# Between gated attention and first experts: the steps of four engines put in a new order, chunk by chunk

## The reference, cut to what matters

```python
x = x + layernorm(L1_attn(layernorm(x)))   # gated attention: sigmoid(s - mu) * exp(s), normalised
x = x + layernorm(L1_ffn(layernorm(x)))    # gated unit: (silu(x @ Wg) * (x @ Wu)) @ Wd, 384 hidden
x = x + layernorm(L2_attn(layernorm(x)))   # linear attention with elu + 1 features, proj, then
                                           # its own LayerNorm, fc1 (512), exact gelu, fc2, residual
x = x + layernorm(L2_ffn(layernorm(x)))    # 16 experts, 4 of them per token, and a shared one
```

## Time and profile before

| | us |
|---|---|
| median of 3 runs (1506.9 to 1511.1) | 1508.39 |
| the profiled execution | 1511.61 |
| its span in the profile | 1509.7 |
| PE busy in the span | 1274.5 (84%) |
| DVE busy | 1133.8 (75%) |
| ACT busy | 1120.9 (74%) |
| POOL busy | 349.2 (23%) |
| last product of the gated attention ends (from the span's start) | 858.0 |
| first matmul of the experts (L2045) starts | 1001.4 |

### The profile page before, as it was taken

The page is one execution under the profiler, slowest core; times in us unless marked ns, Lnnn a source line. Parts: engine busy times, 40 slices in busy tenths (PEclk is TensorE's granted clock), DMA queues, the critical chain, the costliest instruction groups (busy, mean ns, idle before and its releaser), DMA issues.

```text
span 1509.7 us, 22834 instructions
## 1 busy us (share of the span) xinstructions
PE 1274.5 (84%) x8290; PEld 657.9 (44%) x8290; DVE 1133.8 (75%) x2049; ACT 1120.9 (74%) x1604; POOL 349.2 (23%) x434
## 2 busy tenths in 40 slices
PE   6599999885888888888888887788999988888996
PEld 3244444462111111122111245566777866666774
DVE  8888886366697887976779656768756676776898
ACT  4177788747999999999999633455476576877985
POOL 2500001541000000002000034545555557431000
PEclk9599999996899999999999997999999999999998
DMA  5300100004000000100000120013333243011111
GB/s 191 111 24 25 44 24 4 2 5 150 0 22 18 4 22 1 37 21 1 21 1 0 57 92 1 1 31 96 94 112 91 78 112 140 21 36 29 43 50 56
DMA packets 41088, 70.50 MB, mean 47 GB/s; under 512 B 6416, under 2 KB 14864, under 8 KB 40208
## 3 DMA queue, kind: packets, MB, share of 16 engines
q1 hardware_dynamic: 40976, 69.05, 15.0%
HBM read 59.26 MB, written 9.76 MB: 46 GB/s over the span
## 4 chain that ended last, share of the span: by engine, by line
PE 32%; DVE 26%; ACT 20%; issue 13%; POOL 6%; DMA 2%; SPq 1%; POOLq 0%; ACTq 0%; DVEq 0%
ACT SHARED L1144 12%; DVE SHARED L1180 8%; PE PS L823 5%; PE PS L787 3%; PE PS L645 2%; DVE PS L2255 2%; PE PS L712 2%; PE PS L2045 2%; PE PS L2047 2%; PE PS L2046 2%; PE PS L1359 2%; DVE X L284 1%; POOL SHARED L2078 1%; PE PS L2054 1%; DVE STX L266 1%
## 5 line engine op out<-in xcount | busy, mean ns | idle before, releaser
L1144 ACT ACTIVATE SHARED<-PS 128x1536 f32<-128x1536 f32 (+1 forms) x346 | 457.5, 1449 | 14.8 <-PE PS L1036 9.8
L1180 DVE TENSOR_TENSOR SHARED<-SHARED 128x1536 f32<-128x1536 f32 (+1 forms) x170 | 276.6, 1700 | 34.7 <-ACT SHARED L1144 34.7
L1036 PE MATMUL PS<-QS,KS 48*128 48x512 bf16 (+1 forms) x1006 | 208.2, 397 | 83.0 <-ACT SHARED L1144 76.5
L803 ACT ACTIVATE SHARED<-PS 128x512 f32<-128x512 f32 (+3 forms) x384 | 163.6, 493 | 72.1 <-PE PS L791 63.6
L1036 PEld LDWEIGHTS PS<-QS,KS 48*128 48x128 bf16 (+1 forms) x1006 | 38.3, 94 | 297.8 <-ACT SHARED L1144 271.1
L2045 PE MATMUL PS<-ROUNDED 128*128 128x512 f32 x328 | 138.0, 421 | 15.7 <-DVE ROUNDED L2242 7.8
L1049 PE MATMUL PS<-SHARED,Vg 128*16 128x512 f32 x1024 | 139.5, 619 | 7.2 <-DVE SHARED L1180 6.9
L732 DVE TENSOR_REDUCE NM<-PS 128x2 f32<-128x1024 f32 (+3 forms) x128 | 124.0, 1018 | 13.2 <-PE PS L718 12.6
L2047 PE MATMUL PS<-ROUNDED 128*128 128x512 f32 x328 | 130.7, 398 | 0.0
L2046 PE MATMUL PS<-ROUNDED 128*128 128x512 f32 x328 | 130.5, 398 | 0.0
L2175 ACT ACTIVATE ROUNDED<-PS 128x512 fp32r<-128x512 f32 x100 | 59.8, 598 | 91.8 <-DVE PS L2255 91.8
(11 more groups left out here) (279 smaller groups left out, 2483.6 us busy)
## 6 DMA issues: line engine op xcount, KB each, us to landing
SHARED<-wx SPq DMA_DIRECT2D x64, 256.0 KB, 3.2
SHARED<-in_moe SPq DMA_DIRECT2D x3, 1600.0 KB, 10.8
SHARED<-wx SPq DMA_DIRECT2D x16, 224.0 KB, 2.9
SHARED<-kx SPq DMA_DIRECT2D x32, 96.0 KB
KS<-kx SPq DMA_DIRECT2D x32, 96.0 KB
SHARED<-wx SPq DMA_DIRECT2D x16, 192.0 KB, 2.8
SHARED<-wx SPq DMA_DIRECT2D x16, 160.0 KB, 2.8
qx<-SHARED SPq DMA_DIRECT2D x16, 128.0 KB, 2.4
```

Of the source, the lines that this page charges most:

```text
L803: act.activation(PB[t % 3][:, h, q0:CH], bank(RING0[n % 3], q0), ACT.Exp, scale=SCORE_SCALE)\
L1036: ins = pe.matmul(bank((v % 2) * GRP + f - a), KS[g % 2][r, h // 2, kt * P:kt * P + P], QS[g % 2][r, h // 2, qh * CH:(qh + 1) * CH], start ...
L1144: act.activation(dst, PS[:, (v % 2) * GRP * CH:((v % 2) * GRP + b - a) * CH], ACT.Exp if second == qh else ACT.Sigmoid, scale=SCORE_SCALE)\
L1180: dve.tensor_tensor(ex_tile(j), ex_tile(j), GR[w % RING][:, 0:(b - a) * CH], ALU.mult)\
```

## The change

In the gated unit, the single step of a chunk becomes one of a unit: `pe_glu_gate`, `pe_glu_up`, `act_glu` and `dve_glu` now take n, with a semaphore of its own (`gm`) for the gates. The features, `linear_out`, `linear_norm` and the fc1 units are cut up in the same way, with their instructions unchanged. The third job of a chunk gets a bank of its own, 5 or 7, and a matmul waits for the feature three jobs back; T1 and T2 stay two. The last five `pe_weighted1` steps and `pe_out1` move from `pe_gated` into `pe_between`, and the copy and the normalisation of the last half group from `dve_gated` into `dve_between`, so that gates, ups and products stand between them. `late(pe, 1)` ahead of the features is gone, `late(dve, 1)` moves behind them, `late(pool, 2)` and the first splits move ahead of e4's chunk 1. `act_apply` and `act_turned` of e5's chunk 1 move into `act_between`. No instruction that computes is added or taken away.

```diff
-    for kt in range(KT):
-        if WEIGHT_AT[kt] >= NTILE:
-            pe_weighted1(pe, QH * NG - 1, kt)
-    pe_out1(pe, QH * NG - 1)
...
+        if hf + 1 < QH * NG:
+            dve_beside_gated(dve, own, hf + 1)
+            if hf + 1 in QUOTIENT:
+                dve_quotient_begin(dve, own, hf + 1)
+            dve_out1_copy(dve, hf)
+            dve_out1_norm(dve, hf)
+def dve_out1_copy(dve, hf):
+    dve.wait_ge(A[1, "pv"], KT * (hf + 1))
+    if hf:
+        dve.wait_ge(A[1, "ot"], hf)
+    dve.tensor_copy(OS[:, :], bank(6)).then_inc(A[1, "o_sb"], 1)
...
-def pe_glu_up(pe, c):
+def pe_glu_gate(pe, n):
+    c, m = divmod(n, M3)
     pe.wait_ge(h_ready, edges[3].n_x(c))
-    for m in range(M3):
-        n = M3 * c + m
-        if n:
-            pe.wait_ge(A[3, "sg"], n)
-        pe.matmul(bank(2), LF[:, m * P:m * P + P], chunk(hT, c), start=True, stop=True)\
-          .then_inc(A[3, "mm"], 1)
-        if n:
-            pe.wait_ge(A[3, "mul"], n)
-        pe.matmul(bank(3), LF[:, 384 + m * P:384 + m * P + P], chunk(hT, c),
-                  start=True, stop=True).then_inc(A[3, "mm"], 1)
+    if n:
+        pe.wait_ge(A[3, "sg"], n)
+    pe.matmul(bank(2), LF[:, m * P:m * P + P], chunk(hT, c), start=True, stop=True)\
+      .then_inc(A[3, "gm"], 1)
+def pe_glu_up(pe, n):
+    c, m = divmod(n, M3)
+    if n:
+        pe.wait_ge(A[3, "mul"], n)
+    pe.matmul(bank(3), LF[:, 384 + m * P:384 + m * P + P], chunk(hT, c),
+              start=True, stop=True).then_inc(A[3, "mm"], 1)
...
+def act_glu(act, n):
+    act.wait_ge(A[3, "gm"], n + 1)
+    if n >= 2:
+        act.wait_ge(A[3, "mul"], n - 1)
+    act.activation(SG3[n % 2], bank(2), ACT.Silu).then_inc(A[3, "sg"], 1)
+def dve_glu(dve, n):
+    c, m = divmod(n, M3)
+    dve.wait_ge(A[3, "sg"], n + 1)
+    dve.wait_ge(A[3, "mm"], n + 1)
+    if m == 0 and c >= 2:
+        dve.wait_ge(y_ready, YB[3] + c - 1)
+    dve.tensor_tensor(HID3[c % 2][:, m, :], SG3[n % 2], bank(3), ALU.mult)\
+       .then_inc(A[3, "mul"], 1)
...
-    return bank(2 + (3 * c + i) % 2)
+    return bank((2, 3, 5 if c < QH else 7)[i])
...
+def pe_feature(pe, c, i):
     pe.wait_ge(h_ready, edges[4].n_x(c))
-    if c == 0:
-        late(pe, 1)
-    for i in range(3):
-        j = 3 * c + i
-        if c == QH and i < 2:
-            pe.wait_ge(A[4, "o"], 3 + i)
-        elif j >= 2:
-            pe.wait_ge(A[4, "feat"], j - 1)
-        if i == 0:
-            ins = pe.matmul(job_bank(c, i), W[:, WM["q2"], :], chunk(hT, c), start=True, stop=True)
-        for k in range(2 if i else 0):
-            t = TPC * c + 2 * (i - 1) + k
-            ins = pe.matmul(job_bank(c, i)[:, k * 256:k * 256 + 256], tile(hT, t),
-                            W[:, WM["kv2"]:WM["kv2"] + 2, :].rearrange("p a b -> p (a b)"),
-                            start=True, stop=True)
-        ins.then_inc(A[4, "mm"], 1)
+    j = 3 * c + i
+    if j % (3 * QH) >= 3:
+        pe.wait_ge(A[4, "feat"], j - 2)
+    elif i == 2:
+        pe.wait_ge(x_sum, edges[4].n_y(c + 1))
+    elif c == QH:
+        pe.wait_ge(A[4, "o"], 3 + i)
...
+TURNED = ((4, 2), (4, 3), ("4b", 0), ("4b", 1))
 def pe_linear_turn(pe, c):
+    n, k = TURNED[c]
+    pe.wait_ge(h_ready, edges[n].n_x(k))
     pe.wait_ge(A[4, "o"], 2 * c + 2)
```

More of the change, by code:

```diff
@@ new lines, in dve_feature @@
+        def dve_feature(dve, own, c, i):
+            j = 3 * c + i
+            src, t1, t2 = job_bank(c, i), T1[j % 2], T2[j % 2]
+            dst = chunk(QFT, c)
+            if i:
+                at = c * CH + (i - 1) * 256
+                dst = KF[:, at:at + 256].rearrange("p (t e) -> p t e", t=2)
+                src, t1, t2 = pair_view(src, 0), pair_view(t1, 0), pair_view(t2, 0)
+            dve.wait_ge(A[4, "exp"], j + 1)
+            own.link(dve.tensor_scalar(t2, t1, 1.0, None, ALU.min))
+            dve.scalar_tensor_tensor(out=dst, in0=src, scalar=1.0, in1=t2, op0=ALU.add, op1=ALU.max)\
+               .then_inc(A[4, "feat"], 1)
@@ L1710, in act_between @@
[L1710 to L1724 removed]
+            gelu(5)
@@ L2714, in dve_between @@
             e3, e4, e4b, e5 = edges[3], edges[4], edges["4b"], edges[5]
+            last = QH * NG - 1
+            dve_glu(dve, 0)
+            dve_out1_copy(dve, last)
+            dve_glu(dve, 1)
+            dve_out1_norm(dve, last)
+            dve_glu(dve, 2)
             dve_y(dve, own, e3, 2)
+            dve_glu(dve, 3)
+            dve_x(dve, own, e3, 2)
             dve_y(dve, own, e3, 3)
-            dve_glu(dve, 0)
-            dve_x(dve, own, e3, 2)
+            dve_glu(dve, 4)
+            dve_y(dve, own, e4, 0)
@@ L2733, in dve_between @@
-            dve_linear(dve, own, 1)
-            dve_x(dve, own, e4, 3)
-            dve_keep(dve, own, e4, 0)
+            dve_glu(dve, 6)
+            dve_x(dve, own, e4, 0)
+            dve_glu(dve, 7)
+            dve_y(dve, own, e4, 1)
+            dve_glu(dve, 8)
+            dve_glu(dve, 9)
+            dve_x(dve, own, e4, 1)
+            dve_glu(dve, 10)
+            dve_y(dve, own, e4, 2)
+            dve_glu(dve, 11)
+            dve_keep(dve, own, e4, 0)
+            dve_x(dve, own, e4, 2)
@@ L2736, in dve_between @@
+            dve_y(dve, own, e4, 3)
+            dve.memset(VF[:, :, D:D + 1], 1.0)
+            dve_feature(dve, own, 0, 0)
+            dve_feature(dve, own, 0, 1)
+            dve_feature(dve, own, 0, 2)
+            dve_feature(dve, own, 1, 0)
+            dve_feature(dve, own, 1, 1)
+            dve_feature(dve, own, 1, 2)
+            dve_x(dve, own, e4, 3)
+            late(dve, 1)
             dve_kv_blocks(dve, 0)
-            dve_keep(dve, own, e4, 1)
             dve_linear_norm(dve, own, 0)
@@ L2747, in dve_between @@
+            dve_feature(dve, own, 3, 0)
+            dve_feature(dve, own, 3, 1)
+            dve_feature(dve, own, 3, 2)
+            dve_x(dve, own, e4b, 1)
+            dve_kv_blocks(dve, 1)
+            dve_linear_norm(dve, own, 4)
+            dve_linear_norm(dve, own, 5)
+            dve_linear_norm(dve, own, 6)
+            dve_linear_norm(dve, own, 7)
             dve_keep(dve, own, e4, 2)
+            dve_x(dve, own, e4b, 2)
             dve_keep(dve, own, e4, 3)
             dve_clear5(dve, own)
-            dve_x(dve, own, e4b, 2)
+            dve_x(dve, own, e4b, 3)
@@ L2751, in dve_between @@
             dve_y(dve, own, e5, 0)
-            dve_x(dve, own, e4b, 3)
+            dve_x(dve, own, e5, 0)
             dve_y(dve, own, e5, 1)
-            dve_x(dve, own, e5, 0)
             dve_x(dve, own, e5, 1)
```

402 lines of the change are left out of this document (230 added, 172 removed).

## The result

| | before | after |
|---|---|---|
| median of the runs, us | 1509.74 (4 runs, 1506.9 to 1511.6) | 1475.83 (4 runs, 1473.75 to 1478.0) |
| ratio, 95% interval | | 0.9776 (0.976 to 0.9793) |
| the profiled execution, its span | 1511.61, 1509.7 | 1478.0, 1476.2 |
| last gate product starts | 856.8 | 856.7 |
| first expert matmul starts | 1001.42 | 967.27 |

The kernel is 33.9 us faster by the medians and 33.5 by the spans. All of it lies in the distance, which is 34.0 us shorter. This distance is the measure for the experiments too. The work ahead of it is the same in all kernels, but it ends up to 3.4 us earlier or later from one profiled execution to the next, and a median carries that. The part behind the distance is one program in all kernels too; it took 506.1 to 510.2 us in the thirteen profiled executions.

What follows compares the result with a forecast made beforehand. PE's own work, 98 us of 143 between attention and experts, was taken as the floor. The costing gave 34 us; less 1.5 for splits, 3 for clock, 1.5 for hand-overs leaves 28: forecast 1480.4, range 1470 to 1493.

Steps and rivals of the forecast that it cites:

- half of it: Rival: edge statistics come a step late, each of 24 products and features loses 0.65 us; gain 13, time 1495; chance 0.14.
- nothing: Rival: each chunk's chain of edges sets the end; only 1 to 4 us gained, time 1506; chance 0.04.
- slower by the clock: Rival: PE's granted clock falls, a mean of 0.65 giving 158 us in this region, time 1523; chance 0.03.
- The walk: New lists followed instruction by instruction at full clock, attention's end to experts: first expert matmul 967 against 1001.4, gain 34 us.
- Clock in the linear attention: Features and linear attention: a third of the 8.6 us lost before to the clock still lost, 3 us taken off.
- Meetings with the splits: DVE minimums under the features meet POOL's splits: 0 to 5 us, 1.3 in the instruction-by-instruction costing, 1.5 more taken off.
- Hand-overs missed: Whole region: 1.5 us taken off, since PE is 98% full in the costing and 93% in its best stretch before.
- charge of 2 for split 9: Before the experts: split 9 starts together with dve_x of e5 chunk 0; nothing or 2.2 us, taken as 2.
- Weave 1.1: Attention's end: gates 0, 1 and up 0 fill PE's wait; the copy comes earlier, gain 1.1, 2 of 12 units done.
- Gated unit 14 to 15: Gated unit: PE always has work ready, last down ends at 894.5; gain 14 to 15 us, the largest term.
- Third bank: Features: 1.1 us to a matmul's result leaves the loop; rival, T1's two tiles pace them: 4.4 less, time 1485, no separate chance.
- The rule on the shared port: DVE beside POOL's splits: by the rule four meetings cost up to 6 us instead of 2.8, gain 25 instead of 28.

Runs made afterwards that it cites:

- Run 1: Changed kernel with the attention's last steps back ahead of the gated unit on PE, ACT and DVE: 1479.29 us, ratio 0.9808.
- run 2: Changed kernel with feature jobs alternating in two banks again, each matmul waiting for the feature two jobs back: 1479.43 us, ratio 0.9803.
- run 3: Changed kernel with the old order up to the gated unit's last down, attention's end included: 1489.69 us, ratio 0.9868.
- run 4: Changed kernel with the old order from e4 chunk 1 on (features, linear attention, fc1), two feature banks: 1495.57 us, ratio 0.9908.
- run 5: Changed kernel with POOL's split 9 moved from ahead of pool_x of e5 chunk 0 to behind pool_x of e5 chunk 1: 1474.48 us, ratio 0.9769.

## Why the prediction was right

*Forecast 1480.4, range 1470 to 1493; measured 1475.83.* The sign, the range and the mechanism held: PE has work in nearly every place where it waited, and runs 1 to 4, which take parts of the order back, lose the gain again. The size was 5.5 us short by the spans (a gain of 28.0 forecast, 33.5 measured), and the forecast lay 4.6 above the median. The first expert matmul, expected at 970 to 974, came at 967.27. The other cases fell: half of it, nothing, and slower by the clock (0.98, not 0.65). One reading of the old trace was wrong: the 13.1 us in which DVE waits for the up matmul are not time in which PE stands too; PE waited 4.5 us for products.

*The walk.* It gave milestones that the timeline meets within 0.8 us, the last one partly by luck (below): gates 0 and 1 and up 0 between 853.10 and 857.05; `turn_out` at 861.42 (861.45 forecast); the last down ends as the first feature job starts, 895.07 (894.5); `kv` at 903.13 and 920.46 (903.5, 921); the first fc1 unit at 928.67 (929); logits 961.76 (961); experts 967.27 (967). PE was busy 36.32 of 37 us in the gated unit, 98%.

*What failed: the 6 us taken off the walk.* Three deductions, and none was due in full.
- Clock in the linear attention, 3 us. It was granted 1.00 from 895 to 950. The half clock came once, after the pause of 2.20 ahead of 950.00, and cost 5.30 - 3.85 = 1.45. I had charged a third of the old loss for pauses of up to 2.5 us at 903 and 906; there were 1.90 and 0.65. That this charge was not due is partly luck: run 5, with the same pause of 1.91, had half clock behind it, and run 3, with the same order from the features on and a pause of 2.12, was granted 0.90 over 35.6 us, which is 3.6 us.
- Meetings with the splits, 1.5 beyond the walk's 1.3. The twelve minimums took 4.5 us in all, 0.6 more than alone; the keep of 911.01 took 1.2 more and the next 0.3. Together 2.1, and the walk had 1.3 of it.
- Hand-overs missed, 1.5. The walk had nearly all of them.

The walk landed at 967 although it held neither the half clock (1.45) nor 0.8 of the cost of the splits, so it was itself some 2 us too slow elsewhere; without that half clock the kernel would have been at 965.8. Its charge of 2 for split 9 beside the e5 adds was right (1.8), as run 5 shows. The reading that PE is "98% full in the walk and 93% in its best stretch before", and so must lose some, took a measure of the old order for one of the hardware.

*Weave 1.1.* The copy of the attention's result started at 859.09 (859.2 forecast). Run 1 puts the whole weave at 4.4 us; that is close to the 1.1 and the two units done early together, 3.4 at 0.86 for each matmul.

*Gated unit 14 to 15.* What follows the last down starts at 895.07, 14.0 us earlier than 909.09. Run 3, with the old order up to there, has its first feature matmul 12.5 us later than the changed kernel; the kernel before has it 14.4 later, with a longer half clock and one transpose more ahead of it.

*Third bank.* Forecast as 1.1 per job and 4.4 in the rival's price; run 2 measured 4.3 at full clock.

*The rule on the shared port.* The Trainium skill (SBUF — State Buffer, Who interferes with whom) has DVE in a two-port mode, or with two SBUF inputs, and GpSimd lock each other out for a whole instruction. The rows agree in kind: 2.94 against 1.14 for adds with two SBUF inputs, 2.28 against 1.10 for a keep. The price that the prediction worked out from it, a whole subtraction of 1.54 for each of four minimums, was not due, because no minimum started early in a subtraction. The longest, 0.87 instead of 0.42, started at 900.16, and the subtraction beside it ended at 900.74. Before, one took 1.68.
